# Piecewise-linear GELU of a decoder's first feed-forward block: the first rounding moves to ScalarE, the fraction to bit operations on VectorE, and every step runs one piece later

## The reference, cut to what matters

```
def float2fix(x, mantissa_bits):                 # round to multiples of 2^-8
    s = 2.0 ** mantissa_bits
    return round(x * s) / s

def pwlin_gelu_basic(x):
    xq = float2fix(x, 8)
    y  = interp(xq, knots at -4, -3.75, ..., 4, values of exact GELU there)
    y  = where(xq > 4, xq, where(xq < -4, 0, y))
    return float2fix(y, 8)

x = layernorm(x + float2fix(pwlin_gelu(x @ w1 + b1) @ w2 + b2, 8))   # 128 -> 512 -> 128
```

## Time and profile before

| | us |
|---|---|
| median of 3 runs (lowest, highest) | 3427.01 (3425.05, 3427.52) |
| the profiled execution, its own time | 3427.96 |
| its span in the trace | 3426.2 |
| `gelu_phase`: first matmul to the first DMA of the next stage | 1463.5 to 1740.2 |
| mean granted TensorE clock over the span, of 1 | 0.958 |

### The profile page before, as it was taken

The page is one execution under the profiler, slowest core; times in us unless marked ns, Lnnn a source line. Parts: engine busy times, 40 slices in busy tenths (PEclk is TensorE's granted clock), DMA queues, the critical chain, the costliest instruction groups (busy, mean ns, idle before and its releaser), DMA issues. The chain is left out here.

```text
span 3426.2 us, 44444 instructions
## 1 busy us (share of the span) xinstructions
PE 3085.8 (90%) x12374; PEld 1646.6 (48%) x12374; DVE 1765.3 (52%) x2607; ACT 2024.2 (59%) x4072; POOL 1152.1 (34%) x954
## 2 busy tenths in 40 slices
PE   5888888799999999966779999999998879999998
PEld 2333333477777777722234444444444634444443
DVE  5999999455555555589933433333333521111111
ACT  5777776366666666545557777777775523333333
POOL 4788788122222222256623333333332100000000
PEclk8999999799999999988889999999999979999999
DMA  3545544000000000011100000000000300000000
GB/s 97 170 144 167 155 156 149 30 16 21 21 18 21 17 22 17 14 42 52 43 22 14 14 14 14 18 14 14 14 14 31 137 34 19 18 18 28 18 19 12
DMA packets 104265, 159.18 MB, mean 46 GB/s; under 512 B 11904, under 2 KB 44560, under 8 KB 104208
## 3 DMA queue, kind: packets, MB, share of 16 engines
q1 hardware_dynamic: 97872, 144.89, 12.5%
q10 hardware_dynamic: 6336, 13.60, 1.3%
HBM read 85.77 MB, written 4.72 MB: 26 GB/s over the span
## 5 line engine op out<-in xcount | busy, mean ns | idle before, releaser
L1355 POOL TENSOR_TENSOR d_pr<-d_pr,d_keep 128x512 f32<-128x512 f32 x256 | 320.4, 1273 | 566.7 <-ACT d_pr L1513 566.7
L770 POOL TENSOR_TENSOR b_pn<-b_e,b_inv 128x616 f32<-128x616 f32 x128 | 161.4, 1261 | 603.2 <-DVE b_inv L951 603.2
L256 POOL TENSOR_TENSOR a_bx<-a_bcopy,a_drive_u 128x512 f32<-128x512 f32 x256 | 320.2, 1271 | 18.1 <-DVE a_state L523 11.5
L523 DVE TENSOR_TENSOR_SCAN a_state<-a_decay,a_bx 128x512 f32<-128x512 f32 x256 | 311.0, 1215 | 5.7 <-POOL a_bx L256 5.4
L276 PE MATMUL a_py<-a_prod,consts 128*128 128x512 f32 x512 | 285.0, 640 | 2.8 <-DVE a_t L503 1.4
L1922 PE MATMUL f_ph<-f_hb,wb 128*128 128x512 f32 x512 | 232.8, 598 | 6.4 <-ACT f_hb L1955 6.4
L1922 PE MATMUL f_ph<-f_ha,wb 128*128 128x512 f32 x512 | 229.0, 596 | 2.3 <-DVE f_ha L1984 2.3
L454 ACT ACTIVATE a_decay<-a_delta,neg_a 128x508 f32<-128x508 f32 x256 | 174.5, 682 | 73.2 <-DVE a_state L523 73.0
L926 DVE TENSOR_REDUCE b_peak<-b_pscore 128x8 f32<-128x616 f32 x128 | 102.3, 799 | 215.7 <-PE b_pscore L807 215.7
L876 ACT ACTIVATE b_yy<-b_py,y_bias 128x154 f32<-128x154 f32 x512 | 169.4, 382 | 67.8 <-PE b_py L816 67.5
L1577 DVE TENSOR_SCALAR d_ln<-d_pn 128x512 f32<-128x512 f32 (+1 forms) x160 | 101.8, 636 | 197.6 <-PE d_pn L1408 197.6
(11 more groups left out here) (281 smaller groups left out, 6492.0 us busy)
## 6 DMA issues: line engine op xcount, KB each, us to landing
a_bcopy<-rows SPq DMA_DIRECT2D x256, 256.0 KB, 3.5
wb<-in_wb ACTq DMA_DIRECT2D x14, 480.0 KB, 4.2
a_xf<-in_x SPq DMA_DIRECT2D x16, 256.0 KB, 4.2
a_xt<-in_x ACTq DMA_DIRECT2D x16, 256.0 KB, 3.6
x<-a_xo SPq DMA_DIRECT2D x16, 256.0 KB, 2.3
b_xf<-x SPq DMA_DIRECT2D x32, 128.0 KB, 2.0
b_xt<-x SPq DMA_DIRECT2D x32, 128.0 KB, 2.0
x<-b_xo SPq DMA_DIRECT2D x32, 128.0 KB, 2.0
```

The lines of the kernel that those rows point to most:

```text
L256: gp.tensor_tensor(bx[:, k % 4, :], bcopy[:, k % 4, :], drive_u[:, p, :], ALU.mult).then_inc(*bxt.step("bx"))
L523: V.tensor_tensor_scan(state[:, j % 2, :], decay[j % 2][:], bx[:, j % 4, :], 0.0, ALU.mult, ALU.add).then_inc(*vs.step("scan"))
L770: gp.tensor_tensor(heads(pn[:, j % 2, :]), heads(e[:, j % 2, :]), over(inv[:, j % 2, :], CTX), ALU.mult).then_inc(*pnt.step("n"))
L1355: gp.tensor_tensor(half, half, keep[:].unsqueeze(1).to_broadcast([128, QP, SEQ]), ALU.mult).then_inc(*gmt.step(f"m{odd}"))
```

## The change

In words, all of it in `gelu_phase` but the last point:

- The first rounding leaves DVE. b1 comes in by a second matmul into the same PSUM tile (L1126: a row of b1, split in three bfloat16 parts that stand 32 rows apart, times a tile of ones, 96 rows deep), and ACT adds FINE (`Identity` with a bias of one number for each partition, L1156).
- The fraction leaves POOL. DVE makes it with two bit operations in one instruction (L1215): the low six bits of `hb`, put under the exponent of QUARTERS = 1.5 * 2^23 / 64. The product then is `(frac - QUARTERS) * (pg - gl)`, so the factor 4 is gone (L1193).
- `pg - gl` is written back into `pg` in PSUM instead of into `rise` in SBUF (L1189); `ob` is written back into `po` in PSUM (L1198). `rise` and `ob` are gone.
- POOL has only the sum y = frac + gl, and waits before it for the second rounding of the piece before.
- Each step is later: ACT's GELUs stay at lag 1 behind a rounding at lag 0, DVE's masks are at lag 1, the product at lag 3, the second rounding and the second matmul at lag 4. `ob` and `t1` of a group go from the end of the next group's step 3 to step 0 of the group after it, Square and Ln/Exp are both in step 1, and the centre matmul goes from step 0 to the front of step 1. Within a step DVE does first the product, then `ob` and `t1`, then the masks, then the second rounding.
- `prepare_phase` splits b1 into its three parts, two instructions on ACT and two on POOL, and the packed weights are 508 columns wider.

```diff
@@ gelu_phase: gpsimd, tensor
-                        if u := unit(g, k, 1, main, tail):
-                            gp.tensor_tensor(frac[:, j, :], hb[:, j % 2, :], left[:, j % 2, :], ALU.subtract
-                        if u := unit(g, k, 2, main, tail):
+                        if u := unit(g, k, 3, main, tail):
                             pool.wait_ge(*vslope.at("t", r))
+                            if begun(r - 1):
+                                pool.wait_ge(*vround.at("y", r - 1))
...
+                        if late and k == 1:
+                            pe.wait_ge(*vsum.at("s", g - 2))
+                            mm(pc[:], S["center"], t1[:], start=True, stop=True).then_inc(*peo.step("center"))
                         if u := unit(g, k, 0, main, tail):
-                            mm(ph[j % 2][:], W["w1"][:, 128 * j:128 * (j + 1)], xf[:, p, :], start=True, stop=True
+                            mm(ph[j % 2][:], W["w1"][:, 128 * j:128 * (j + 1)], xf[:, p, :], start=True, stop=False)
+                            mm(ph[j % 2][:], S["b1"][:, 128 * j:128 * (j + 1)], ones[:], start=False, stop=True
                                ).then_inc(*peh.step("h"))
-                        if late and k == 0:
-                            mm(pc[:], S["center"], t1[:], start=True, stop=True).then_inc(*peo.step("center"))
                         if late and k == 1:
                             mm(pv[:], S["mean"], t2[:], start=True, stop=True).then_inc(*peo.step("var"))
-                        if u := unit(g, k, 3, main, tail):
+                        if u := unit(g, k, 4, main, tail):
                             pe.wait_ge(*vround.at("y", r))
@@ scalar
+                        if late and k == 1:
+                            A(t2[:], pc[:], ACT.Square).then_inc(*so.step("sq"))
+                        if u := unit(g, k, 0, main, tail):
+                            act.wait_ge(*peh.at("h", r))
+                            A(hb[:, j % 2, :], ph[j % 2][:], ACT.Identity, bias=offset[:]).then_inc(*fixed.step("x"))
                         if u := unit(g, k, 1, main, tail):
                             A(gl[:, j, :], left[:, j % 2, :], ACT.Gelu, bias=at_left[:]).then_inc(*knots.step("left"))
                             A(pg[j % 2][:], left[:, j % 2, :], ACT.Gelu, bias=at_right[:]
-                        if late and k == 0:
-                            A(t2[:], pc[:], ACT.Square).then_inc(*so.step("sq"))
-                        if late and k == 2:
+                        if late and k == 1:
                             nc.scalar.preload_act_table_set("natural_log_exp_and_others")
@@ vector
-                            V.tensor_scalar(hb[:, j % 2, :], ph[j % 2][:], W["b1"][:, j:j + 1], FINE, ALU.add, ALU.add
+                        if u := unit(g, k, 3, main, tail):
+                            dve.wait_ge(*knots.at("right", r))
+                            V.tensor_tensor(pg[j % 2][:], pg[j % 2][:], gl[:, j, :], ALU.subtract
+                            V.scalar_tensor_tensor(out=frac[:, j, :], in0=frac[:, j, :], scalar=QUARTERS,
+                                                   in1=pg[j % 2][:], op0=ALU.subtract, op1=ALU.mult
+                        if late and k == 0:
+                            dve.wait_ge(*pe2.at("o", FC * (g - 1) - 1))
+                            V.tensor_scalar(po[p][:], po[p][:], W["b2"], FINE, ALU.add, ALU.add
+                            V.scalar_tensor_tensor(out=t1[:], in0=po[p][:], scalar=FINE, in1=xt[:, p, :],
+                        if u := unit(g, k, 1, main, tail):
+                            dve.wait_ge(*fixed.at("x", r))
                             V.tensor_scalar(left[:, j % 2, :].bitcast(I32), hb[:, j % 2, :].bitcast(I32), -KNOTS, None,
+                            V.tensor_scalar(frac[:, j, :].bitcast(I32), hb[:, j % 2, :].bitcast(I32), KNOTS - 1,
+                                            QUARTERS_BITS, ALU.bitwise_and, ALU.bitwise_or).then_inc(*vfix.step("f"))
+                        if u := unit(g, k, 4, main, tail):
+                            V.tensor_scalar(y[:, j % 2, :], y[:, j % 2, :], FINE, FINE, ALU.add, ALU.subtract
```

More of the change, by code:

```diff
@@ L590, in _ @@
                 op.then_inc(*made.step("f3"))
+            @block.scalar
+            def _(act):
+                act.wait_ge(S["background"], 32 * PARTS)
+                nc.scalar.activation(S["b1"][:], W["b1_rows"], ACT.Copy).then_inc(*held.step("hi"))
+                act.wait_ge(*split.at("rest", 0))
+                nc.scalar.activation(S["b1"][0:64, :], rest[0:64, :], ACT.Copy).then_inc(*held.step("mid"))
+            @block.gpsimd
+            def _(pool):
+                pool.wait_ge(*held.at("hi", 0))
+                nc.gpsimd.tensor_tensor(rest[:], W["b1_rows"], S["b1"][:], ALU.subtract).then_inc(*split.step("rest"))
+                pool.wait_ge(*held.at("mid", 0))
+                nc.gpsimd.tensor_tensor(S["b1"][0:32, :], rest[0:32, :], S["b1"][0:32, :], ALU.subtract
+                                        ).then_inc(*split.step("lo"))
+                pool.wait_ge(*split.at("lo", 0))
             @block.vector
@@ L970, in gelu_phase @@
     KNOTS = 64
+    QUARTERS = 1.5 * 2 ** 23 / 64
+    QUARTERS_BITS = 0x48400000
     xres = S["x"]
@@ L1005, in gelu_phase @@
         store = ctx.enter_context(nc.semaphore("c_store"))
-        set_up = tr("set_up", "left right")
+        set_up = tr("set_up", "left right offset ones")
         peh = tr("peh", "h")
         knots = tr("knots", "left right")
-        vfix = tr("vfix", "x left")
-        pfrac = tr("pfrac", "f")
+        fixed = tr("fixed", "x")
+        vfix = tr("vfix", "left f")
         vslope = tr("vslope", "d t")
@@ L1154, in _ @@
                 V.memset(at_right[:], 0.25 - FINE).then_inc(*set_up.step("right"))
+                V.memset(offset[:], FINE).then_inc(*set_up.step("offset"))
+                V.memset(ones[:], 1.0).then_inc(*set_up.step("ones"))
                 def step(g, p, main, tail, late):
@@ new lines, in step @@
+                            V.tensor_tensor(pg[j % 2][:], pg[j % 2][:], gl[:, j, :], ALU.subtract
+                                            ).then_inc(*vslope.step("d"))
+                            dve.wait_ge(*vfix.at("f", r))
+                            dve.wait_ge(*vslope.at("d", r))
+                            V.scalar_tensor_tensor(out=frac[:, j, :], in0=frac[:, j, :], scalar=QUARTERS,
+                                                   in1=pg[j % 2][:], op0=ALU.subtract, op1=ALU.mult
+                                                   ).then_inc(*vslope.step("t"))
@@ L1190, in step @@
                             V.tensor_tensor(xo[:, p, :], pc[:], t3[:], ALU.mult).then_inc(*vo.step("out"))
-                        if tail and k == 3:
-                            dve.wait_ge(*pe2.at("o", FC * g - 1))
-                            V.tensor_scalar(ob[:], po[1 - p][:], W["b2"], FINE, ALU.add, ALU.add
-                                            ).then_inc(*vobround.step("o"))
-                            dve.wait_ge(*vobround.at("o", g - 1))
-                            dve.wait_ge(load_t, 16 * g)
-                            if begun(g - 2):
-                                dve.wait_ge(*peo.at("center", g - 2))
-                            V.scalar_tensor_tensor(out=t1[:], in0=ob[:], scalar=FINE, in1=xt[:, 1 - p, :],
-                                                   op0=ALU.subtract, op1=ALU.add).then_inc(*vsum.step("s"))
                 drive3(dve, step)
```

75 lines of the change are left out of this document (36 added, 39 removed).

## The result

| | before | after |
|---|---|---|
| median of 15 runs (lowest, highest), us | 3426.47 (3417.85, 3432.33) | 3435.08 (3427.11, 3444.09) |
| profiled execution: its time, its span | 3427.96, 3426.2 | 3427.14, 3425.4 |
| `gelu_phase`, first matmul to the next stage's first DMA | 1463.47 to 1740.20: 276.7 | 1460.47 to 1743.38: 282.9 |
| granted TensorE clock over the span | 0.958 | 0.956 |

The account below looks back on a forecast made before the run. VectorE set the pace before; afterwards a ring through TensorE, ScalarE and VectorE would. Start -6.1, turns +7.6 and last group +0.4 gave +1.9 on 3427.96, 3429.9, on the runs' scale 3429 us; range 3404 to 3446.

Parts of the forecast that it names:

- first product to first `t1`: Start of `gelu_phase`: the first `t1` comes at 1484.7 instead of 1490.85, 6.1 us earlier.
- 14 turns: Steady part of `gelu_phase`, first to fifteenth `t1`: 14 groups of 17.0 us, 238.0 against 230.4, +7.6 us.
- fifteenth to sixteenth `t1`: Last group: 9.4 us before; 9.1 at 2.4 GHz or 10.5 at 1.2, taken as 9.8, +0.4.
- to the next stage: From the sixteenth `t1` to the next stage's start: 9.5 us as before, no change.
- The ring: Closed chain of waits through TensorE, ScalarE and VectorE (3.0, 6.6, 5.7 us) sets each group's turn: 15.3 us at 2.4 GHz.
- The clock: TensorE falls to 1.2 GHz after waits on the ring: 0 to 2.8 us a group, taken as 1.7, turn 17.0.
- clock stays up: Rival: TensorE stays at 2.4 GHz on the ring; turn 15.3, -22.6 us, 3404 us; chance 0.17.
- the whole ring slow: Rival: 1.2 GHz for w2(0), centre, ph(1), b1; 2.8 us a group, turn 18.1, 3445 us; chance 0.25 together with dear masks.
- The masks: VectorE's mask and fraction take 0.43 us each; rival: the median's 0.5 more on four, turn 17.3 with the clock up.
- `prepare_phase`: Two added copies on ScalarE and two operations on GpSimd, some 4 us: cost nothing, or 4 us if last.
- The unclosed ring: Rival: a wait has more slack, so the fullest engine sets the pace at 11.8 us a group; 3356 us; chance 0.08.

Follow-up runs that it names:

- e1: Changed kernel plus five unused matmuls per group in TensorE's waits, three ahead of w2(3), two ahead of w2(0); 3408.32 us, ratio 0.9939 to before.
- e4: Kernel before plus three unused matmuls per group in TensorE's wait for `t1`, ahead of the centre product; 3427.65 us, ratio 1.0001.
- e5: Changed kernel with centre product and Square moved to step 0 and the Ln/Exp block to step 2; 3427.16 us, ratio 1.0002 to before.
- e9: e5 plus three unused products ahead of the centre product, in TensorE's wait for `t1`; 3390.29 us, ratio 0.9882 to before.
- e2: Changed kernel with the centre product moved to step 0, ahead of w2(0); 3405.91 us, ratio 0.9929 to before.
- e12: Changed kernel with the variance product placed behind w2(1) in step 1 instead of ahead of it; 3429.43 us, ratio 0.9999 to before.
- e10: e5 with the bias sum and `t1` ahead of the normalising product `xo` on VectorE; 3386.27 us, ratio 0.9869 to before.
- e11: e10 plus two unused products ahead of the centre product on TensorE; 3376.22 us, ratio 0.9857 to before.
- e8: e5 plus three unused products on TensorE ahead of w2(3); 3432.03 us, ratio 1.0016 to before.
- e6: e2 plus three unused products on TensorE ahead of w2(3); 3398.04 us, ratio 0.9916 to before.
- e7: Changed kernel without both table loads per group, Ln and Exp replaced by Identity, output not normalised as the reference's; 3390.30 us, ratio 0.9903 to before.

## Why the prediction was right, point by point

| term | predicted | measured in the trace |
|---|---|---|
| first product to first `t1` | -6.1 | 22.33 against 27.38: -5.05 |
| 14 turns | 14 x 17.0: +7.6 | 238.06 against 230.42: +7.64 |
| fifteenth to sixteenth `t1` | +0.4 | 12.12 against 9.43: +2.69 |
| to the next stage | 0 | 10.40 against 9.50: +0.9 |
| sum | +1.9 | +6.2 |

- **The ring.** Its links were right. VectorE's 5.7 us measured 5.68, ScalarE's 6.6 (with the signal to `left`) 5.86 + 0.72 = 6.58, TensorE's 3.0 + 1.7 of clock 1.86 + 1.82 + 1.15 = 4.83. At 2.4 GHz it was given as 15.3; the first turn of after takes 15.22 (1482.80 to 1498.02), before the slow clock has set in, and e1's average is 15.40.
- **The clock.** The taken price of 1.7 us a turn measured 17.00 - 15.40 = 1.6. e4 shows that it cost nothing before. The rival "clock stays up" was a real branch, but needs work that is not in the kernel; "the whole ring slow" had too much: in the turn shown w2(0) (2.08 us) and most of the centre product (1.78) were slow, and ph(1) behind them was back at 2.4 GHz (1.02). The estimate came from half the work of one slow window, and that it fits so well is partly luck: in e5's order the clock cost 2.3 us a turn (16.68 against e9's 14.34), in e2's 0.3.
- **The masks.** They are as cheap as taken:

```profile
L1211 DVE TENSOR_SCALAR c_left<-c_hb x64: 415/426/532, 1463.8 to 1721.5; 128x512 int32<-128x512 int32 x64
```

By tile as in the earlier trace rows. The median is 0.43 us, where before it was 0.93, and the one in most groups that overlaps GpSimd's sum by 0.2 us takes 0.53. Results written to PSUM cost hardly more (`pg - gl` 0.69 against 0.68, bias sum 0.75 against 0.73).
- **What was off.** The mis-sized term is the fifteenth to the sixteenth `t1`, "taken as 9.8": 12.1. I had let sums and roundings follow each other and left out the order on TensorE, where w2(1) waits behind a product of the output step; e12 shows it, and leaves 10.3. Behind it 0.9 is the slow clock: the last group's centre product takes 2.08 us, before 1.12, and the variance product 2.07 in both. At the start 1.05 less was gained than forecast; why was not looked into. Together these make the 4.3 us between +1.9 and +6.2. The steady turns, to which 238 of the stage's 283 us belong, were off by less than 0.1 in all. On the scale of the runs the forecast would have been 3433, close to the 3435 measured. The remaining 2 us lie within what the unchanged stages differ by between the two profiled executions (7.0 us).
- **`prepare_phase`.** 17.5 us before (640.09 to 657.59) and after (636.51 to 654.02): hidden, as predicted.
- **The unclosed ring** (3356 us) was called an order that I did not see. e10 (3386 us) and e11 (3376) come nearer to it by moving `t1` ahead of the normalising product. It needs the change of order as well as the lighter VectorE.

So the change did take 66 us of VectorE's work and 80 of GpSimd's out of the steady stretch. None of it came out as time, because the same edit put the centre product, Square and the Ln/Exp block in one ring with rounding(2), and because the slow clock lies on that ring. Mending one of the two already helps: the clock held up gives 3408 us (e1), the centre product ahead of w2(0) 3406 (e2). With the three steps as before, but the clock low, the time stays (e5, 3427); with TensorE kept busy as well the lighter kernel is 40 us faster than before (e9). Rounding(1) and rounding(2) on ScalarE are themselves links of the ring, 0.60 and 0.73 us; no run gives them back to VectorE alone.

## What to carry to other kernels

When a change takes the bound off an engine, look for the closed chains of waits that go through several engines and add up each by start-to-start distances, in steady turns and once more for the last group, before crediting the freed time: the longest one sets the turn. Moving a step later is not free even if every engine has room, since each move can close such a chain. The clock that fell in waits was free while VectorE was full (e4) and a link when it was not (e1). Products of no use held it up at a gain where they filled a wait that ended later than they did (e1, e9), and at a loss ahead of what another engine waited for (e8).

## What the runs showed of the hardware

- The slow clock comes late: in the turn of after, w2(3) behind a wait of 3.10 us is still 1.13 us long, the next product 1.80, w2(0) 2.08. In e5 the product behind a wait of 4.26 us is 2.07 long at once. Three to five products of no use kept the granted clock at 1.00 over 200 us (e1, e4, e6, e9), where they filled waits of the group. In e8 three took 4.54 us in most turns, against 2.74 in e6 and e9: they can run slowly themselves.
- The integer mask on VectorE took 0.93 us where it ran beside GpSimd's sum `y`, and 0.43 without it, though the instruction is the same. Before, in order of time, the sum, the mask and the fraction, which waits for the mask and starts behind it:

```profile
1603.38 1.27 POOL L1085 TENSOR_TENSOR c_y<-c_frac,c_gl 128x512 f32<-128x512 f32 x1 [0.63 <-DVE c_frac L1170]
...
1604.00 0.93 DVE L1184 TENSOR_SCALAR c_left<-c_hb 128x512 int32<-128x512 int32 x1
...
1605.09 1.27 POOL L1078 TENSOR_TENSOR c_frac<-c_hb,c_left 128x512 f32<-128x512 f32 x1 [0.44 <-DVE c_left L1184]
```

58 of before's 64 masks overlap the sum by 0.6 to 0.7 us and take 0.93 to 1.02. In after one instruction of the same form, a fraction (L1215) that lies wholly beside the sum, takes 1.49 us against 0.42 for the 63 others. Otherwise the sum there runs mostly beside `pg - gl` and the product. So the masks of after are cheap because the sum runs at another time, as the prediction had it, and not because the fraction left GpSimd. That is read from the overlaps; no run moves the sum alone. The product is dear beside GpSimd's fraction instead: before, 0.86 to 1.18 us in the 46 that overlap it by 0.3 us or more, 0.69 in the other 18. Its mean first before (1545 to 1700 us), then after (1463.47 to 1740.2; count, busy us, mean ns, idle before):

```profile
L1170 DVE SCALAR_TENSOR_TENSOR c_frac<-c_frac,c_rise 128x512 f32<-128x512 f32 x38 | 34.4, 906 | 3.6 <-DVE c_rise L1166 1.3
```

```profile
L1193 DVE SCALAR_TENSOR_TENSOR c_frac<-c_frac,c_pg 128x512 f32<-128x512 f32 x64 | 44.0, 688 | 3.9
```

With one operand in PSUM it takes 0.69 us every time, also in the 33 that overlap GpSimd's sum by 0.7 us.
- A table load cost its 1.28 us and 0.01 or 0.02 more: in all steady turns of after the next instruction started 1.29 or 1.30 us after the load's start, and without both loads a turn at the same clock was 2.8 us shorter (e7, 15.22 to 12.41).
